# Spreading and interleaving the late output step on GpSimd in a fused attention and coupled-FFN kernel

## The reference, cut to what matters

```python
def attention(query, ctx, mask, W_out, scale, log_C):      # 16 heads of 16
    u = einsum('hbqd,hbkd->hbqk', q, k) * scale / sqrt(16)
    attn = softmax(where(mask, -inf, tanh(u) * exp(log_C)))  # 120 keys
    return heads(attn @ v) @ W_out.T

def ffn(x):
    gf = global_net(x.mean(axis=1))                         # 3 layers
    out = x
    for _ in range(3):
        coupling = 0.1 + adaptive_range * (0.7 * gf + 0.3 * coupling_net(out) - 0.5) * 2.0
        o_r, o_i, p_r, p_i = split(out, 4)
        out = out + coupling * concatenate([p_r, -p_i, -o_r, o_i])
    return out

x = x + attention(layernorm(x), ctx, ctx, mask, W_out, scale, log_C)
x = x + ffn(layernorm(x))
```

## Time and profile before

| | |
|---|---|
| median of 3 runs | 1132.01 us |
| runs | 1126.67, 1132.01, 1135.17 us |
| the profiled execution | 1132.01 us, span 1130.2 us |
| mean granted TensorE clock | 0.970 |
| busy, share of the span | PE 88%, ACT 82%, DVE 72%, POOL 53% |

### The profile page before, as it was taken

The page is one execution under the profiler, slowest core; times in us unless marked ns, Lnnn a source line. Parts: engine busy times, 40 slices in busy tenths (PEclk is TensorE's granted clock), DMA queues, the critical chain, the costliest instruction groups (busy, mean ns, idle before and its releaser), DMA issues.

```text
span 1130.2 us, 21970 instructions
## 1 busy us (share of the span) xinstructions
PE 996.0 (88%) x7260; PEld 537.7 (48%) x7260; DVE 814.6 (72%) x1738; ACT 924.7 (82%) x1153; POOL 596.1 (53%) x1117
## 2 busy tenths in 40 slices
PE   7889988899888998889989898899988999886993
PEld 4555435554355544554345543555435554353431
DVE  4888486966688686885859849598586966677285
ACT  4999778987699877997779977799778986795576
POOL 4577406982169802797048940498305982068204
PEclk7999999999999999999999999999999999999897
DMA  4121001210022100220002200122001210001002
GB/s 123 42 56 33 1 2 60 76 52 1 1 70 73 44 1 2 88 75 24 1 20 94 67 8 2 47 71 70 1 1 57 80 51 1 1 29 39 10 1 76
DMA packets 67280, 43.85 MB, mean 39 GB/s; under 512 B 42080, under 2 KB 50784, under 8 KB 67168
## 3 DMA queue, kind: packets, MB, share of 16 engines
q1 hardware_dynamic: 67168, 42.45, 13.2%
HBM read 25.51 MB, written 16.78 MB: 37 GB/s over the span
## 4 chain that ended last, share of the span: by engine, by line
PE 32%; ACT 20%; POOL 18%; DVE 16%; issue 13%; DMA 0%; POOLq 0%; DVEq 0%; SPq 0%; ACTq 0%
ACT probs L878 7%; PE ps L1186 6%; PE ps L1199 6%; ACT probs L884 5%; PE ps L1110 5%; PE ps L1173 4%; POOL twisted L507 3%; DVE move_u L766 3%; POOL f_hat L452 2%; PE ps L1141 2%; PE ps L1229 2%; DVE coup L732 2%; POOL va L432 2%; DVE move_u L745 2%; PE ps L1208 2%
## 5 line engine op out<-in xcount | busy, mean ns | idle before, releaser
L878 ACT ACTIVATE probs<-ps,u_scale 120x2048 f32<-120x2048 f32 x128 | 254.0, 1984 | 33.5 <-PE ps L1110 33.3
L884 ACT ACTIVATE probs<-probs,exp_bias,clip 120x2048 f32<-120x2048 f32 x128 | 270.4, 2112 | 0.1
L1199 PE MATMUL ps<-h,w 128*128 128x512 f32 x384 | 184.2, 605 | 14.9 <-ACT h L910 14.1
L1110 PE MATMUL ps<-q_t,k_t 32*120 32x256 f32 x2048 | 156.6, 422 | 43.4 <-ACT probs L878 42.6
L471 POOL TENSOR_TENSOR c<-tok_c 128x16 f32<-128x16 f32 x8 | 1.8, 223 | 329.6 <-issue 329.6
L1141 PE MATMUL ps<-wo_t,of_t 128*128 128x256 f32 x512 | 149.0, 415 | 2.8 <-DVE xy L701 2.8
L676 DVE STREAM_TRANSPOSE o_t<-ps 128x512 f32<-128x512 f32 x128 | 90.8, 709 | 79.9 <-PE ps L1126 79.3
L1126 PE MATMUL ps<-probs,va 120*32 120x256 f32 x2048 | 139.5, 391 | 5.6 <-ACT probs L884 5.6
L1110 PEld LDWEIGHTS ps<-q_t,k_t 32*120 32x120 f32 x2048 | 98.6, 189 | 74.2 <-issue 68.8
L1141 PEld LDWEIGHTS ps<-wo_t,of_t 128*128 128x128 f32 x512 | 90.1, 196 | 60.9 <-issue 49.9
L1199 PEld LDWEIGHTS ps<-h,w 128*128 128x128 f32 x384 | 66.8, 188 | 90.4 <-issue 65.3
(11 more groups left out here) (129 smaller groups left out, 1858.4 us busy)
## 6 DMA issues: line engine op xcount, KB each, us to landing
xy<-in_x_dram SPq DMA_DIRECT2D x64, 256.0 KB, 2.7
out_dram<-xy SPq DMA_DIRECT2D x64, 256.0 KB, 2.0
cbuf<-in_ctx_dram SPq DMA_DIRECT2D x64, 120.0 KB, 2.2
tok_c<-coup SPq DMA_DIRECT2D x256, 0.5 KB, 2.0
move_v<-in_L_xattn_W_out_dram SPq DMA_DIRECT2D x1, 256.0 KB, 5.4
move_u<-in_L_ffn_cn_w_dram SPq DMA_DIRECT2D x1, 256.0 KB, 5.7
w<-in_L_ffn_cn_w_dram SPq DMA_DIRECT2D x1, 128.0 KB, 5.7
g<-in_L_ffn_gc_w_dram SPq DMA_DIRECT2D x1, 128.0 KB, 4.1
```

The lines of the kernel that those rows point to most:

```text
L878: eng.activation(probs[:, b % 2, n * HALF:(n + 1) * HALF, :].rearrange("k h q -> k (h q)"), banks(SCORE_BANK, 4)[0:KEYS, :], ACT.Tanh, sca ...
L884: eng.activation(p, p, ACT.Exp, scale=clip[0:KEYS, 0:1], bias=exp_bias[:, b:b + 1]).then_inc(s_exp, 1)
L1110: last = eng.matmul(banks(SCORE_BANK + r)[0:KEYS, odd * S:(odd + 1) * S], k_t[rows, b % 2, odd, n, :], q_t[rows, b % 2, n, :], start=True, ...
L1199: last = eng.matmul(banks(bank), w2[:, k, :], h1[:, p % 2, k, :], start=(k == 0), stop=(k == EK - 1))
```

## The change

The change is in POOL's program alone. In a slot other than position 0 it now goes: `twisted_part`, `norm_2_scale`, `x_part`, `norm_2`, `query_scale`, `values`, `query_hat`; before it was `norm_2_scale`, `query_scale`, `norm_2`, `twisted_part`, `x_part`, `values`, `query_hat`. In position 0 it takes one late batch instead of two, so that each of the eight positions has one, and POOL's late batch is that of DVE's `combine` in the same slot.

```diff
-                if 0 <= i - LAG < NB:
+                if after_ffn(i):
+                    if i - LAG < NB:
+                        norm_2_scale(i - LAG)
+                        norm_2(i - LAG)
+                    coefficients(groups_before(i) - 1)
+                for b in late[:1]:
+                    twisted_part(b)
+                if 0 <= i - LAG < NB and not after_ffn(i):
                     norm_2_scale(i - LAG)
+                for b in late[:1]:
+                    x_part(b)
+                late = late[1:]
+                if 0 <= i - LAG < NB and not after_ffn(i):
+                    norm_2(i - LAG)
                 if new is not None and 2 <= new < NB:
                     query_scale(new)
-                if 0 <= i - LAG < NB:
-                    norm_2(i - LAG)
-                if after_ffn(i):
-                    coefficients(groups_before(i) - 1)
-                for b in late[:2] if after_ffn(i) else late[:1]:
-                    twisted_part(b)
-                    x_part(b)
-                late = late[2:] if after_ffn(i) else late[1:]
                 if 0 <= i + 1 < NB:
                     values(i + 1)
```

## The result

The changed kernel takes 1144.76 us (median of four runs, 1141.7 to 1146.03) against 1129.7 us of the kernel before beside it: a ratio of 1.0124, 95% interval 1.0075 to 1.0174. It is slower by 15 us where 1 us was forecast, and its median stands 0.8 us above the upper end of the range. The profiled execution has a span of 1142.4 us, 12.2 more than before.

The account below looks back on a forecast made before the run. POOL was taken to bound the stretch from 330 to 363 us, ACT position 5. Five groups at -0.3, group 3 +0.5 and tail +1.9 sum to +0.9 us on 1132.01: 1132.9, written 1133.0; range 1124 to 1144.

Parts of the forecast that it names:

- part d: DVE's `combine` waits anew for POOL's x part behind the scale; in position 4 PE is held 0.5 us for k_t.
- q_hat's wait: Position 6: PE's 1.76 us wait for q_hat goes, with its slow clock; such a slot was 2.3 us too long.
- The tail: After the last attention slot, the end comes 1.35 to 2.4 us later; 1.9 us taken, paid fully.
- the loop: Scale, x part, `combine`, k_t, then `stats_2` to the next scale: 8.15 us, 8.75 with the cast, beside ACT's 8.40.
- the stretch: POOL and DVE operations lengthened beside each other: 0.4 us more in three of five positions, turning the gain into +0.3 loss.
- The prediction's own walk through group 2: Positions 2 to 7 timed undisturbed: PE held 0.5 us in position 4, position 7's last transposes 0.9 us earlier.
- -0.3 us per group: Five groups each change by -0.3 us, between the undisturbed and the disturbed sum; ends: 2.3 gained or 1.5 lost.
- Group 3: Its q_hat wait taken as about half the others', 1.2 us, so it ends +0.5 us.
- The port rule: `combine` beside N pays up to 0.55 us per linked position: group +1.3, kernel near 1142; clock or port loss 0.16.
- Full relief: Only the wait for q_hat goes, DVE's new waits fall in idle time: 1121.2 us; chance 0.17, wholly or by half.
- The slower rival: Waits for k_t in positions 4 and 6 cost PE its clock, 0.95 us each: 1144.3 us; clock or port loss 0.16.
- the third rival: q_hat stays late in its slot and the loop only adds: +5.5 us, 1137.5 us; chance 0.12.

Follow-up runs that it names:

- e1_combine_last: The changed kernel with `combine` at the end of DVE's slot in all positions: 1118.37 us, ratio 0.9921 to the kernel before.
- e3_x_first: The changed kernel with the x part directly behind the twisted part, ahead of norm 2's scale: 1115.33 us, ratio 0.9895 to the kernel before.
- f3_combine_behind_kt: The changed kernel with `combine` directly behind `keys_out` on DVE: 1124.65 us, ratio 0.9957 to the kernel before.
- g2_small_combine: The changed kernel with `combine` over 8 of every 64 columns, output incomplete, all waits kept: 1123.12 us, ratio 0.995 to the kernel before.
- e2_interleave_ahead: The changed kernel's order inside a slot, but two late batches in position 0 and none in position 7: 1119.62 us, ratio 0.993 to the kernel before.
- f1_spread_only: The kernel before with one late batch in each position, its order inside a slot unchanged: 1312.4 us, ratio 1.1619 to the kernel before.
- g1_x_first_tail: e3_x_first with two late batches in position 0 of the last group only: 1117.68 us, ratio 0.9903 to the kernel before.

## Why the prediction was right or wrong

**The mechanism** (part d) was right up to PE: `combine` waits for an x part behind the scale, most in position 4, and k_t ends after PE wants it. The slow clock behind q_hat's wait is gone, the wait itself only by half (0.83 us, and 0.82 in position 7). The tail is longer by 1.9 us, the term of the sum, though that was a value picked between 1.35 and 2.4. Taking `combine` out of k_t's way or the x part out of the scale's took all of the loss away (e1_combine_last, e3_x_first), and moving k_t alone ahead of `combine` most of it (f3_combine_behind_kt).

What (d) calls the loop, 8.15 us from scale to scale through the statistics, is not what set the pace where the time was lost. In positions 4, 6 and 7 the scale starts 1.8 us after its statistics; POOL's own work sets it. That work is 9.88 us in a slot with q_hat and low_half, and without the stretch of f_hat (0.43) and `values` (0.53) still 8.9, beside ACT's 8.4. The kernel before had the same: 9.34 us from the scale of position 5 to that of position 6. There it cost q_hat's wait alone, since the late batch was one slot ahead; spreading it put `combine`, and with it k_t, behind this queue. The prediction's own walk through group 2 does have POOL late in position 4, so the numbers below are right; the comparison of 8.15 with 8.40 is not what they hang on.

**The term that failed** is the stretch. I priced the loop at 8.15 us undisturbed, 8.75 with the cast, called its reserve hardly any, and then entered -0.3 us per group, "between the undisturbed and the disturbed sum", with 0.4 us of disturbance in three positions. Measured is +2.0 (+2.8 in group 3, where +0.5 was forecast). In position 3 POOL lost 0.43 on f_hat and 0.53 on `values`, so `low_half` ended 2.4 us after the slot's first tanh and not 1.7; in position 4 `combine` took 0.97 us from start to start of the next operation, not 0.75. Together k_t came 8.2 us after the first tanh of slot 4, where I had 7.3 and PE needs it by about 6.8. The same happened in positions 6 and 7. Where POOL has no pause and k_t hangs on it, every such piece goes straight into the time; a middle between two sums was the wrong value to take, because nothing in this chain could take up a stretch.

**Group 3** was priced on a misreading: its wait for q_hat was not half of the others', it was the same 1.76 us, and only the slow clock behind it was missing.

**The port rule.** The rule of the Trainium skill, page "SBUF — State Buffer" ("Who interferes with whom"), that a VectorE instruction with two SBUF inputs and a GpSimd instruction that reads SBUF hold one pair of ports exclusively, each for the whole instruction, was weighed in the prediction, with a sum of +1.3 for a group and a time near 1142. That was the better sum: 2.0 and 1144.8 were measured, and in g2_small_combine an operation of 0.19 us that takes 0.47 and ends with f_hat's half agrees with an exclusive lock. I had set it aside in favour of a T of 1.53 us that seemed to show half of it. The 1.53 was no half: of T's two operations one took 0.56 us and the other, held, 0.99; in position 4 both halves of f_hat were longer (0.83 and 1.23). In part the sum was close by luck, though. It let `combine` pay up to 0.55 us; `combine` paid 0.22, and the rest was paid on POOL, by f_hat and `values`, which that price left out.

**The rivals.** Full relief did not come. The slower rival had the place right (k_t of positions 4 and 6) and the result nearly (1144.3), but for a reason that fell: PE's clock. PE stood 1.66 us for k_t and the window shows a granted clock of 1.00 there, so the sum came near by luck. It had rested on a stand of 1.76 us bringing the slow clock, which group 3 of the kernel before already contradicts. The change did relieve q_hat, so the third rival fell too, though the relief was half of what I had (PE stands 0.83 us there still).

**Spreading and order.** They were one change and have opposite effects: the order alone gains 0.7% (e2_interleave_ahead), the spreading alone costs 16% (f1_spread_only), both together cost 1.2%. The prediction has no sum for either of them by itself.

What stays open: how much of the 2.0 us per group is stretch and how much POOL's bare work with k_t behind it. g2_small_combine shortens `combine` as well as it frees the ports, and no run here does one without the other. Whether g1_x_first_tail really gains its 3.5 us at the end is open as well.

## What to carry to other kernels

When a producer is moved from one step ahead of its consumer to the same step, write down two lengths: the ring of waits that now closes, every handoff in it, and the producer's own work from one such step to the next. Compare both with the period of the engine that sets the pace. The ring decided in f1_spread_only (12.7 us against 8.4), the producer's own work in the changed kernel (9.9 against 8.4). A producer that falls behind in some steps and catches up in others needs the distance that the change takes away. Then take what the pace hangs on out from behind it at the cheapest place: here the x part in front of three small operations, with no instruction added, turned 1.2% slower into 1% faster. In such a chain price operations of VectorE and GpSimd that start together at their stretched length.

## What the runs showed of the hardware

- `combine` over an eighth of its elements, on VectorE: 0.19 us for the first operation, whose record starts 0.06 us behind that of GpSimd's f_hat, 0.47 us for an equal one 0.11 us later (g2_small_combine). Shortening one of two operations in conflict does not shorten its wait. And which of two is held can't be told from a difference of 0.06 us in their starts: here f_hat, recorded first, did not hold the first operation.
- The stretch goes both ways, and to more than two instructions: f_hat's two halves 1.10 us alone, 1.53 beside `combine`, 2.05 with the cast behind it; `values` 0.87 to 1.39; an operation of `combine` 0.42 to 1.38 beside `low_half`.
- A stand of PE of 1.66 us for k_t was followed by scores of 1.14 us at a granted clock of 1.00, a stand of 3.44 us in f1_spread_only by scores of 2.08. In the kernel before, the same stand of 1.76 us at the same place was followed by scores of 2.08 in five groups and of 1.14 in group 3. The length of one stand alone doesn't tell which clock level follows.
- Two remedies for the same wait did not add: by their ratios e1_combine_last is 9 and e3_x_first 12 us faster than the kernel before, both together only 6.
